# Stored turned rows for the later shared tiles of a mixture-of-experts layer (one core, Trainium2)

## The reference, cut to what matters

```python
x = x + ffn(layernorm(x))                            # twice in the network
def ffn(x):                                          # x: 4096 x 256 normalised rows
    probs = softmax(x @ gate_w.T)                    # router, 8 experts
    topk_w, topk_i = top_k(probs, 2); topk_w /= sum(topk_w)
    eo[t, e] = (silu(x @ w_gate[e]) * (x @ w_up[e])) @ w_down[e]    # 256 -> 352 -> 256
    out = sum over the two chosen experts of topk_w * eo
    sg = sigmoid(x @ shared_gate_w.T)
    return out + sg * ((silu(x @ sw_gate) * (x @ sw_up)) @ sw_down)  # the shared expert, all rows
```

## Time and profile before

| | us |
|---|---|
| median of 3 runs | 1940.58 |
| lowest and highest | 1935.58, 1942.81 |
| span of the profiled execution, first to last instruction | 1946.8 |
| PE busy (share of the span) | 1855.2 (95%) |
| VectorE (DVE), ScalarE (ACT), GpSimd (POOL) busy | 1348.6, 1179.6, 416.6 |
| bytes moved by DMA | 149.13 MB, mean 77 GB/s |

### The profile page before, as it was taken

One profiled execution on the slowest core, in us unless ns is written; L12 is line 12 of the kernel. 1 busy time (PEld: TensorE's weight loads), 2 busy tenths in 40 slices (PEclk: granted clock), 3 DMA queues, 4 the chain that ended last, 5 costly groups with the idle time before them and its releaser, 6 DMA issues. The chain is left out here.

```text
span 1946.8 us, 51759 instructions
## 1 busy us (share of the span) xinstructions
PE 1855.2 (95%) x19836; PEld 1437.6 (74%) x19836; DVE 1348.6 (69%) x2724; ACT 1179.6 (61%) x2371; POOL 416.6 (21%) x497
## 2 busy tenths in 40 slices
PE   6998899999999888999999999999998999999998
PEld 5677789999999654465555555565545789999997
DVE  6555678544445877899999999999944877444445
ACT  5211354554545544799889988989895644445443
POOL 1121100455553333000000000000000002555541
PEclk9999999999999999999999999999999999999999
DMA  7000121222225665312122111111005211222228
GB/s 303 1 1 0 39 76 29 66 79 74 80 71 170 153 180 150 89 42 54 44 55 49 42 41 41 41 42 41 3 3 200 100 36 35 78 76 79 74 65 265
DMA packets 86539, 149.13 MB, mean 77 GB/s; under 512 B 35620, under 2 KB 69284, under 8 KB 80612
## 3 DMA queue, kind: packets, MB, share of 16 engines
q1 hardware_dynamic: 68428, 103.24, 17.6%
q0 software_dynamic: 17856, 42.60, 7.9%
q10 hardware_dynamic: 24, 0.02, 0.0%
HBM read 96.68 MB, written 48.76 MB: 75 GB/s over the span
## 5 line engine op out<-in xcount | busy, mean ns | idle before, releaser
L2201 ACT ACTIVATE att_scores_pt<-att_scores_psE 128x512 f32<-128x512 f32 x1024 | 598.1, 597 | 68.6 <-PE att_scores_psE L1705 26.3
L1720 DVE TENSOR_REDUCE att_mx<-att_scores_psS 128x1 f32<-128x1024 f32 x472 | 578.1, 1225 | 49.8 <-PE att_scores_psS L1705 18.5
L1705 PE MATMUL att_scores_psE<-att_qs,att_ks 99*32 99x512 bf16 x4096 | 438.1, 382 | 3.9 <-DVE att_scores_psO L2231 3.1
L2303 PE MATMUL att_scores_psO<-att_scores_pt,att_va 128*17 128x256 f32 x4096 | 330.5, 379 | 2.9 <-ACT att_scores_osb L2206 1.3
L1705 PE MATMUL att_scores_psS<-att_ks,att_qs 96*32 96x512 bf16 x3776 | 308.8, 380 | 0.1
L1705 PEld LDWEIGHTS att_scores_psE<-att_qs,att_ks 99*32 99x32 bf16 x4096 | 137.0, 95 | 102.8 <-ACT att_scores_pt L2201 8.8
L2303 PEld LDWEIGHTS att_scores_psO<-att_scores_pt,att_va 128*17 128x17 f32 x4096 | 132.5, 98 | 102.3 <-issue 13.2
L658 DVE TENSOR_TENSOR moe_hidT_rest<-moe_ps,moe_hidT_high 128x384 fp32r<-128x384 f32 x142 | 79.2, 558 | 184.9 <-ACT moe_hidT_high L377 172.2
L865 PE MATMUL moe_ps<-W_rest,moe_srcT_high 128*128 (+2 forms) x824 | 200.3, 324 | 0.0
L283 POOL DMA_INDIRECT expert_rows<-work,moe_slots_i x142 | 140.0, 986 | 218.8 <-issue 108.1
L1705 PEld LDWEIGHTS att_scores_psS<-att_ks,att_qs 96*32 96x32 bf16 x3776 | 127.1, 98 | 77.0 <-issue 1.3
(11 more groups left out here) (327 smaller groups left out, 3146.3 us busy)
## 6 DMA issues: line engine op xcount, KB each, us to landing
W_gate_up<-in_gate_up_dram SPq DMA_DIRECT2D x2, 6346.0 KB, 21.8
work<-expert_rows SPq DMA_DIRECT2D x12, 1024.0 KB, 7.9
query_key_parts<-att_qkv_parts SPq DMA_DIRECT2D x64, 192.0 KB, 2.8
normalised_rows<-work SPq DMA_DIRECT2D x64, 128.0 KB, 1.9
att_qs<-query_key_parts SPq DMA_DIRECT2D x16, 384.0 KB, 4.4
att_ks<-query_key_parts SPq DMA_DIRECT2D x16, 384.0 KB, 4.5
W_down<-in_down_a_dram SPq DMA_DIRECT2D x2, 2304.0 KB, 28.1
work<-normalised_rows SPq DMA_DIRECT2D x36, 128.0 KB, 2.1
```

Source lines behind the costliest of these rows:

```text
L1705: last = nc.tensor.matmul(out[j:j + 32, :], stationary[:, j:j + 32], moving, start=True, stop=True, tile_position=(0, j), skip_group_check ...
L1720: return nc.vector.tensor_reduce(a.mx[g % 2][:, v:v + 1], bank[:, :, :].rearrange("p h k -> p (h k)"), AX.X, ALU.max)
L2201: nc.scalar.activation(pt[s % 2][:, r, :], psE[use % E_BANKS][:, :], ACT.Exp, scale=HD ** -0.5).then_inc(p_ready, 1)
L2303: last = nc.tensor.matmul(psO[32 * r:32 * r + VC, cols], va[g][:, kt, r * VC:(r + 1) * VC], pt[s % 2][:, r, cols], start=(kt == 0 and part ...
```

## The change

Turned rows of tiles 4 to 31 are kept. `extra_T` becomes seven buffers instead of two; SP stores each turned tile to a new HBM tensor `turned_rows` (after the stores of the next look step's group), and `extra_out` waits for the store of seven tiles before. The 18 shared tiles of the ring are loaded from `turned_rows` instead of `kept`; the ten late ones are loaded by DMAs that ACT issues in place of its activation. For these 28 tiles PE makes no transposes; `source_out` copies from the loaded buffer, after a wait for the load and for the end of the gate/up before (`u_done`), and `source_rest` subtracts from the same buffer. Buffers of the ring come free with `srcT_split` instead of `T_done`, also for POOL's first fetches. `choose_second` waits for all turned stores, since its tables lie where `extra_T` lay. `late_shift` is gone.

```diff
--- before
+++ after
@@ -86,7 +86,7 @@
         extra_src = [work[:, 13 + u, :] for u in range(BESIDE)]
-        extra_T = [work[:, 20 + u, :].rearrange("p (k t) -> p k t", k=KD) for u in range(2)]
+        extra_T = [work[:, at, :].rearrange("p (k t) -> p k t", k=KD) for at in (20, 21, 24, 25, 26, 27, 28)]
         eq, pk0, pk1, lg2, both = [work[:, 22 + u, :].rearrange("p (t e) -> p t e", e=E) for u in range(5)]
@@ -109,7 +109,6 @@
         D_high = [in_work(f"down_high{k}", (12 + 8 * k) * D, [P, E, D]) for k in range(KI)]
-        late_shift = sb("late_shift", [P, NT - NA])
         FIRST = LOOK + BESIDE
@@ -154,6 +153,7 @@
         x_stored = [sem(f"x_stored{u}") for u in range(BESIDE)]
+        T_stored = [sem(f"T_stored{u}") for u in range(BESIDE)]
         early_loaded = [sem(f"early_loaded{u}") for u in range(SRC - 2)]
@@ -167,7 +167,7 @@
         hot_ready = sem("hot_ready"); lane_done = sem("lane_done")
-        late_ready = sem("late_ready"); late_scale = sem("late_scale")
+        late_loaded = [sem(f"late_loaded{u}") for u in range(LATES)]
         got_loaded = [sem(f"got_loaded{g}") for g in range(GOT)]
@@ -177,6 +177,9 @@
         buffer = lambda n: (src[n % 2] if n < LOOK else src[ring(n)] if n < NA else src[(n - NA) % SRC] if n < LAST else late_src[(n - LAST) % LATES])
+
+        turned = lambda n: n < LOOK or kind(n) == "routed"
+        turns = lambda n: n + 1 if n < LOOK else LOOK + n - NA + 1
@@ -202,18 +205,26 @@
         @block.sync
         def _(sp):
+            def turned_rows(n):
+                for x in range(n * BESIDE, (n + 1) * BESIDE):
+                    sp.wait_ge(x_srcT, x + 1)
+                    sp.dma_start(xt_d[:, x, :], extra_T[x % BESIDE].rearrange("p k t -> p (k t)")).then_inc(T_stored[x % BESIDE], 16)
+
             for n in range(LOOK):
                 sp.wait_ge(src_ready, n + 1)
                 sp.dma_start(kept[:, n, 0:D], src[n % 2][:, 0:D]).then_inc(xn_stored[n % 2], 16)
                 for x in range(n * BESIDE, (n + 1) * BESIDE):
                     sp.wait_ge(x_src, x + 1)
                     sp.dma_start(kept[:, LOOK + x, 0:D], extra_src[x % BESIDE]).then_inc(x_stored[x % BESIDE], 16)
+                if n:
+                    turned_rows(n - 1)
+            turned_rows(LOOK - 1)
             for n in range(LOOK, NA):
                 x = n - LOOK
-                sp.wait_ge(x_stored[x % BESIDE], 16 * (x // BESIDE + 1))
+                sp.wait_ge(T_stored[x % BESIDE], 16 * (x // BESIDE + 1))
                 if n >= LOOK + SRC - 2:
-                    sp.wait_ge(T_done, n - (SRC - 2) + 1)
-                sp.dma_start(src[ring(n)][:, 0:D], kept[:, n, 0:D]).then_inc(early_loaded[ring(n) - 2], 16)
+                    sp.wait_ge(srcT_split, n - (SRC - 2) + 1)
+                sp.dma_start(src[ring(n)][:, 0:D], xt_d[:, x, :]).then_inc(early_loaded[ring(n) - 2], 16)
                 if n == LOOK + 11:
                     sp.wait_ge(cw_ready, 1)
                     sp.dma_start(kept[:, :, D:XW], cw[:, :, :]).then_inc(cw_stored, 16)
@@ -270,7 +281,7 @@
                 elif j >= 2:
-                    pool.wait_ge(T_done, max(n for n in range(LOOK, NA) if ring(n) == j) + 1)
+                    pool.wait_ge(srcT_split, max(n for n in range(LOOK, NA) if ring(n) == j) + 1)
                 nc.gpsimd.indirect_dma_start(
@@ -339,7 +350,9 @@
                 act.wait_ge(x_T, x + 1)
-                nc.scalar.copy(extra_T[x % 2][:, :, :].rearrange("p k t -> p (k t)"), psX[x % BESIDE % 2][:, 0:D]).then_inc(x_srcT, 1)
+                if x >= BESIDE:
+                    act.wait_ge(T_stored[x % BESIDE], 16 * (x // BESIDE))
+                nc.scalar.copy(extra_T[x % BESIDE][:, :, :].rearrange("p k t -> p (k t)"), psX[x % BESIDE % 2][:, 0:D]).then_inc(x_srcT, 1)
@@ -352,20 +365,26 @@
             def source_out(n, u):
-                act.wait_ge(T_done, n + 1)
-                nc.scalar.copy(srcT_high[u].rearrange("p k t -> p (k t)"), psT[:, 0:D]).then_inc(srcT_ready, 1)
+                high = srcT_high[u].rearrange("p k t -> p (k t)")
+                if turned(n):
+                    act.wait_ge(T_done, turns(n))
+                    nc.scalar.copy(high, psT[:, 0:D]).then_inc(srcT_ready, 1)
+                    return
+                if n < NA:
+                    act.wait_ge(early_loaded[ring(n) - 2], 16 * ((n - LOOK) // (SRC - 2) + 1))
+                else:
+                    act.wait_ge(late_loaded[(n - LAST) % LATES], 16 * ((n - LAST) // LATES + 1))
+                act.wait_ge(u_done, n)
+                nc.scalar.copy(high, buffer(n)[:, 0:D]).then_inc(srcT_ready, 1)
             def late_rows(l):
                 n, t = LAST + l, NA + l
-                if l == 0:
-                    act.wait_ge(late_scale, 1)
                 if l < LATES:
                     act.wait_ge(hid_ready, NA + (NB - 1 - l) // SRC * SRC + l + 1)
                 else:
-                    act.wait_ge(T_done, n - LATES + 1)
-                nc.scalar.activation(late_src[l % LATES][:, 0:D], X[:, t, :], ACT.Identity, bias=late_shift[:, l:l + 1],
-                                     scale=rstd[:, t:t + 1]).then_inc(late_ready, 1)
+                    act.wait_ge(srcT_split, n - LATES + 1)
+                nc.scalar.dma_start(late_src[l % LATES][:, 0:D], xt_d[:, t - LOOK, :]).then_inc(late_loaded[l % LATES], 16)
             def silu_step(n, u):
                 act.wait_ge(g_done, n + 1)
@@ -480,7 +499,7 @@
                 dve.wait_ge(srcT_ready, n + 1)
-                nc.vector.tensor_tensor(srcT_rest[u].rearrange("p k t -> p (k t)"), psT[:, 0:D],
+                nc.vector.tensor_tensor(srcT_rest[u].rearrange("p k t -> p (k t)"), psT[:, 0:D] if turned(n) else buffer(n)[:, 0:D],
                                         srcT_high[u].rearrange("p k t -> p (k t)"), ALU.subtract).then_inc(srcT_split, 1)
@@ -543,6 +562,8 @@
             def choose_second():
+                for u in range(BESIDE):
+                    dve.wait_ge(T_stored[u], 16 * (EX // BESIDE))
                 nc.vector.scalar_tensor_tensor(lg2[:, :, :], pk[0][:, :, :], -3.0e38, lg[:, :, 0:E], ALU.mult, ALU.add)
@@ -756,7 +777,6 @@
                 step(n, "shared", finding.get(n, (lambda: one_hots(i)) if 0 <= i < CH // PIECE else None))
-            nc.vector.scalar_tensor_tensor(late_shift[:, :], mv[:, NA:, 0], -1.0, rstd[:, NA:], ALU.mult, ALU.mult).then_inc(late_scale, 1)
             for n in range(NA, LAST):
@@ -800,7 +820,7 @@
                 for k in range(KD):
-                    last = nc.tensor.matmul(psL[:, x * (E + 1):(x + 1) * (E + 1)], extra_T[x % 2][:, k, :],
+                    last = nc.tensor.matmul(psL[:, x * (E + 1):(x + 1) * (E + 1)], extra_T[x % BESIDE][:, k, :],
                                             router[:, k, 0:E + 1], start=(k == 0), stop=(k == KD - 1))
@@ -825,15 +845,11 @@
                 if k == "routed":
                     pe.wait_ge(src_loaded[loaded[0]], loaded[1])
-                elif k == "late":
-                    pe.wait_ge(late_ready, n - LAST + 1)
-                elif n < LOOK:
+                else:
                     pe.wait_ge(src_ready, n + 1)
-                else:
-                    pe.wait_ge(early_loaded[ring(n) - 2], 16 * ((n - LOOK) // (SRC - 2) + 1))
                 if not (isinstance(n, int) and n == 0):
                     pe.wait_ge(srcT_split, n)
-                if isinstance(n, int) and 0 < n <= LOOK:
+                if isinstance(n, int) and 0 < n < LOOK:
                     pe.wait_ge(x_srcT, n * BESIDE - 1)
                 transpose_rows(psT, b).then_inc(T_done, 1)
@@ -943,7 +959,8 @@
                     down(n - 1, (n - 1) % 2, SHARED, "shared" if n >= 2 else None)
-                rows_in(n + 1, buffer(n + 1), "shared", None)
+                if n + 1 < LOOK:
+                    rows_in(n + 1, buffer(n + 1), "shared", None)
@@ -962,13 +979,9 @@
                     look_step(n)
                     return None, here_e
                 gate_up(n, here % 2, here_e)
-                if here + 1 < NS:
-                    nk = kind(here + 1)
-                    loaded = None
-                    if nk == "routed":
-                        j = here + 1 - NA
-                        loaded = (j % SRC, (j // SRC + 1) * 16)
-                    rows_in(n + 1, buffer(here + 1), nk, loaded)
+                if kind(here + 1) == "routed":
+                    j = here + 1 - NA
+                    rows_in(n + 1, buffer(here + 1), "routed", (j % SRC, (j // SRC + 1) * 16))
                 if TABLES + 2 <= here < TABLES + 2 + CH // PIECE:
                     inverse(here - TABLES - 2)
                 if here == LOOK + 3:
...
+        xt_d = nc.dram_tensor("turned_rows", [P, NT - LOOK, D], F32).ap()
```

(2 more changed lines are left out.)

4 lines of the change are left out of this document (2 added, 2 removed).

## The result

The kernel after takes 1954.45 us (median of 4 runs, 1952.01 to 1957.59) where the kernel before, run beside it, takes 1939.24 (4 runs, 1935.58 to 1942.81): 15.2 us more by the medians. The ratio of the runs is 1.0073, 95% interval 1.0055 to 1.0091, which is 14.2 us. The forecast was 14.5 us slower, 1955. The profiled execution after has a span of 1954.4 us, against 1946.8. Such steps come with the change as well as without it (experiments 4 and 11). So the profiles are compared stretch by stretch.

A forecast was written before the change was run, and what follows sets the result against it. PE, busy 95% of the span, was taken as the bound, with DMA also full in the late steps; -4.0 + 1.4 + 1.0 + 10.1 + 6.0 = +14.5 us gave 1955 us, 8-in-10 range 1936 to 1964.

The forecast's parts named there:

- Pairs of transposes in the shared steps, -4.0: Tiles 5 and 11 to 19: ten of 18 pairs count, 2.0 us saved a call, -4.0 us in both.
- Tile 4, +1.4: Tile 4's turned load lands late, so its gate/up starts 0.7 us late a call, +1.4 us in both.
- The first steps, +1.0: Look steps: ACT's first copy may wait for turned stores, 0 to 1.7 us a call, taken as 0.5, +1.0 in both.
- Late steps, first call, +10.1: Loads slowed to L = 6.4 hold four late steps at 6.85 us: 12.1 lost less 2.0 from pairs, +10.1 us.
- my upper bound: Late loads' highest L: 2.1 + 3.2 for turns + 2.7 of starting wait, gives 8; +13 us in the first call.
- No slack at the end of the first call: End of the first call: nothing taken off, so the late steps' +10.1 us counts in full.
- Late steps, second call, +6.0: Late steps lose the first call's 10.1 us, less 4.1 of slack before the last store: +6.0 us (0 to +9).
- The sum: Whole kernel: -4.0 + 1.4 + 1.0 + 10.1 + 6.0 = +14.5 us.
- Late loads unhindered: Rival: late tile loads pass the large loads without delay, sum -3.6 us, 1937 us; chance 0.22.
- Turns alone, L = 4.7: Rival: late loads only take turns by packet, with no wait at the start; sum +5.1 us, 1946 us; chance 0.14.
- The faster rival: VectorE's chain shrinks with PE, so every pair counts, also in the choosing steps: -10.4 us, 1930 us; chance 0.08.
- Look steps losing at each store: Rival: ACT waits for stores in all three look steps a call, +10.8 us on the forecast, 1965 us; chance 0.05.

The follow-up runs named there:

- experiments 4 and 11: The kernel before, unchanged, profiled a second and a third time: a span of 1949.7 us beside a median of 1949.28, then 1949.64 us.
- after_again: The kernel after, unchanged, run again on another chip: 1951.98 us beside 1940.63 of the kernel before, ratio 1.0074.
- before_third: The kernel before, unchanged, profiled a third time: 1949.64 us.
- late_old: The kernel after with its ten late tiles remade by ACT and transposed on PE as before: 1948.14 us, ratio 0.9990 to the kernel before.
- nine_places: The kernel after with nine late-tile buffers, nine tiles loaded by SP before the results, early stores in turn: 1936.37 us, ratio 0.9984 to the kernel before.
- before_stores: The kernel before with the output's stores in another order, a control: ratio 0.9981 to the kernel before.
- nine_stores: nine_places with the output's stores reordered (groups 0, 1, 4 to 7, then 2, last tile, 3): ratio 0.9982 to the kernel before.

## Why the prediction was right, point by point

- **Pairs of transposes in the shared steps, -4.0.** Measured -2.4 and -2.8 a call (after_again's 73.96 against 76.40 in before_third, 73.54 against 76.34), -5.2. The count held: 412 row transposes for 524. The ten pairs that I counted (tiles 5 and 11 to 19) gave 2.0 us a call, as forecast, most of them 0.21 to 0.23 each. The rest is in steps that I had left out: those of tiles 6, 9 and 20 won 0.22 to 0.24 each and the one into the routed stretch 0.3 to 0.4, against that of tile 10, which lost 0.43 and 0.10. So VectorE's chain doesn't set all the choosing steps. Where it does, the wait for its X update did grow, by more than the 0.2 I named; beside the earlier trace rows:
```profile
297.77 1.53 PE L930 MATMUL moe_ps<-W_down,work 128*128 128x256 f32 x6 [1.48 <-DVE X L699]
```
- **Tile 4, +1.4.** Its silu step went from 8.17 us to 9.34 and 8.74 (8.92 and 8.71 the second time), 0.5 to 1.2 a call, +1.7 and +1.3 for both. The copy waited 3.07 us for the load; its base was ACT idling anyway.
```profile
273.24 0.40 ACT L378 CAST moe_srcT_high<-work 128x256 fp32r<-128x256 f32 x1 [3.07 <-DMA work<-turned_rows]
```
- **The first steps, +1.0.** At full clock only the third of the second call lost, 9.42 to 10.06 us (9.94 again): +0.5 to 0.6. With tile 4 that is +2.4 and +1.8, some +2.1, where I had +2.4; the rest of the difference in the first column of the table is steps at a lower clock. The run late_old, with the same stores, lost 0.7 us at full clock in its first step (8.65 for 7.94), so the term varies from one execution to the next, as forecast.
- **Late steps, first call, +10.1.** Ten steps measured 48.80 and 47.88 against 37.52: +11.3 and +10.4. L, the time from a load's issue to its landing, was 6.1 on the mean of five where I took 6.4 for four. Its parts are those I named, a wait at the start (some 2.5 us in the first slow load, 2.7 in my upper bound) and turns (8 records an engine, 3.2 in my upper bound): 2.6 beside the 1 MB loads, but under 1 us for a load like that of 616.64, beside the accumulates. The step's form was wrong: I added 0.45 us for copy and semaphore, but the queue takes the next load beside the copy (609.35 and 609.38 above), so a step is L itself. Five steps at 6.1 and four at 6.85 come to much the same sum (12.5 and 13.0 us over 3.6 a step), so two errors cancelled, which is luck. The lower clock of the gate/up behind a wait (0.88 over the stretch) cost nothing more: the next load was on its way by then.
- **No slack at the end of the first call.** I had put this at nothing, and it failed. The call ended 8.0 to 10.3 us after its last silu, now 6.85. Before, the last accumulate landed at 642.70, and GpSimd's drain instruction of 3.66 us and the barrier behind it let the attention start at 647.79; in the kernel after it landed at 639.95, and the last silu came at 646.85. So 1.1 us (3.4 against before_third) came back.
- **Late steps, second call, +6.0.** This term was mis-sized: +15.3 and +15.9 on the ten steps, because the contention holds six loads of 6.6 us there, where I carried over the first call's 10.1. The output's stores, which the first call lacks, are the likely reason; no run leaves them out. The slack I read from the earlier trace rows as 4.1 was 4.6 to 5.3 (8.77 and 8.42 against 13.37 to 13.75). Net +10.3 to +10.8.
- **The sum**, with after_again against before_third: -5.2 + 2.1 + (10.4 - 3.4) + (15.8 - 5.1) = +14.6. By the ratios +14.2 and +14.4 were measured. The sum leaves out the routed stretch, where before_third has 6.8 us more of long steps, and what lies outside the two calls, 3.8 us more in before_third; with these the two spans differ by only 3.3 us, so the agreement rests on taking both as not owed to the change. The forecast's +14.5 has the late part of the second call 4 to 5 us too low, that of the first up to 3 too high, and 1.2 too little gain in the shared steps. The mechanism, late loads that land late with one in flight, was right; that the total fits to a few tenths of a us is luck.
- **The rivals.** Late loads unhindered: no; they land in 2.0 to 2.8 us until the 1 MB loads start, then in 5 to 9. The Trainium skill (DMA: Bandwidth & Descriptors, "Queues, rings and completion order") has an engine drain a packet of some 9 to 17 descriptors before it switches, by which 8 descriptors would go at once. The trace doesn't agree: of the load of 609.38, 115 data records had moved by 615.30, in turns with the 8 KB records, and no engine had finished its eight. The rival fails on both counts, the wait and the turns. Turns alone, L = 4.7: no, the first record of a slow load starts 2.4 to 3.9 us after the issue instead of 1.0. The faster rival needed PE's waits for VectorE to stay at 0.80: they grew. Look steps losing at each store: no, though ACT did wait for stores five and six times in the two profiles (5.5 and 8.7 us).

## What to carry to other kernels

A load that replaces work on an idle engine is priced by its latency in the busiest window it falls in, not by its median: 128 KB took 2.0 us on the median and 5 to 9 beside the 1 MB loads and the accumulates. With one load in flight every step is as long as that. Count the steps of lead before the change is made: one step more made the same loads nearly free. And where a gain is to come at the end of a stage, look first at what else ends there: nine places took 3.7 us out of the late steps of the kernel before, and at the end of the second call alone the exchange of results took 3.3 of them back (16.86 for 13.52).

## What the runs showed of the hardware that I had not expected

- A small load beside large ones waits twice: its first record started some 3.5 us after the issue instead of 1.0, and then each of its 8 records an engine took a turn with one 8 KB record of the other queue (115 against 107 in 2.45 us).
- Two small loads in flight lengthen each other only by a quarter (means of 7.8 against 6.1 us in the first call, 8.3 against 6.6 in the second), so throughput rises although latency does.
- TensorE's granted clock falls in gaps made by such waits. Stretches of the kernel after: one full wait, then the step behind it; then the last long wait and the step behind that.
```profile
612.50:616.60 4.10, 1.94 (x11) 1.49 (x10) 0.52 (x1) 0.00 (x0) 2.68 (x2) 1.00 1.03 389
616.60:618.90 2.30, 1.81 (x7) 1.81 (x8) 1.83 (x3) 0.86 (x3) 0.00 (x0) 0.71 0.94 267
618.90:622.10 3.20, 3.20 (x14) 2.93 (x14) 1.87 (x3) 0.45 (x1) 0.00 (x0) 0.68 1.22 211
...
630.20:635.20 5.00, 2.24 (x12) 1.50 (x10) 1.77 (x3) 0.00 (x0) 0.00 (x0) 0.94 1.12 288
635.20:637.90 2.70, 2.20 (x7) 2.20 (x8) 2.15 (x4) 0.89 (x3) 0.00 (x0) 0.50 1.02 404
```
PE did 1.94 of 4.1 us and 2.24 of 5.0 us of work, and the gate/up behind ran at a granted clock of 0.71 (part of it at 1.2 GHz) and 0.50 (all of it). From ACT's copy to the next silu it took 2.3 and 2.6 us, against 1.7 behind the two shorter waits between them, where the granted clock was 1.00.
- The first two steps of a call run at a granted clock of 1.00 in some executions and at 0.76 to 0.84 in others, 1.1 to 1.8 us a step; in three calls the second step was at 0.56 to 0.61 and took 13.5 to 14.3 us for 9.4. The kernel before, unchanged, shows both 7.94 and 9.01 us for the first step, so the edits aren't needed for it. Whether the turned stores make it more frequent is open: with the stores as in the kernel after, 11 of 14 profiled calls start so, in the kernel before and before_stores 3 of 8, and the three steps of 13.5 us and more are all among the 11.
- The last 512 KB accumulate took 7.5 us in nine_places and 14.1 in nine_stores, where stores of the output go beside it.
